# Decay attention: value product in two halves, diagonal block in two pairs, unread matmuls in the filling

## What is computed

```python
scores = jnp.einsum('bhqd,bhkd->bhqk', qh, k_rec) / math.sqrt(d)
t = jnp.arange(s, dtype=jnp.float32)
decay = jnp.exp(-LAMBDA_DECAY * jnp.abs(t[:, None] - t[None, :]))
scores = scores * decay[None, None, :, :]
attn = jax.nn.softmax(scores, axis=-1)
out = jnp.einsum('bhqk,bhkd->bhqd', attn, v_rec)
```

## Time and profile before

| | |
|---|---|
| median of 3 runs | 1181.23 us (1179.67 to 1182.42) |
| the profiled execution's own time | 1183.64 us |
| its span | 1181.8 us |
| PE busy | 1059.1 us (90%) |
| DVE busy | 768.1 us (65%) |
| ACT busy | 648.9 us (55%) |
| decay attention, filling to last step | 241 to 700 us of the span |

### The profile page before, as it was taken

How to read it: one execution, slowest core, us unless ns; L and a number is a source line. 1 busy time by engine, 2 the same in 40 slices (tenths; PEclk the granted TensorE clock), 3 DMA queues, 4 the chain that set the end, 5 groups by cost and what they waited for, 6 DMA issues and landing times.

```text
span 1181.8 us, 14237 instructions
## 1 busy us (share of the span) xinstructions
PE 1059.1 (90%) x5214; PEld 397.2 (34%) x5224; DVE 768.1 (65%) x1234; ACT 648.9 (55%) x1098; POOL 185.6 (16%) x107
## 2 busy tenths in 40 slices
PE   5899998985999999999999999998899758999998
PEld 2233333331233333333333334443343212344343
DVE  2678236368899999999998221026599998973200
ACT  4687455272277877877777652335744374413321
POOL 0222810033000000000000000000164313450000
PEclk9899999995599999999999999999899978999999
DMA  7000000069633032130000000000000000000000
GB/s 257 1 2 1 0 0 1 5 240 279 134 55 57 7 60 41 23 61 4 7 8 3 6 1 0 1 0 1 0 1 1 1 0 1 0 1 1 18 0 18
DMA packets 31194, 38.24 MB, mean 32 GB/s; under 512 B 7964, under 2 KB 22300, under 8 KB 30744
## 3 DMA queue, kind: packets, MB, share of 16 engines
q1 hardware_dynamic: 31128, 37.37, 12.5%
HBM read 23.23 MB, written 13.86 MB: 31 GB/s over the span
## 4 chain that ended last, share of the span: by engine, by line
PE 59%; ACT 11%; DVE 10%; issue 3%; DMA 1%; SPq 1%; ACTq 0%; DVEq 0%; POOL 0%; another core or an unknown queue 0%
PE PS L1437 17%; PE PS L1030 11%; PE PS L1014 8%; ACT arena L1039 6%; DVE ffn L926 3%; PE PS L1426 2%; PE PS L1446 2%; PE PS L1427 2%; PE PS L994 2%; DVE arena L1660 2%; PE PS L1071 1%; PE PS L916 1%; PE PS L1602 1%; PE PS L1612 1%; DVE arena L1543 1%
## 5 line engine op out<-in xcount | busy, mean ns | idle before, releaser
L926 DVE CUSTOM_DVE_ANT_0 ffn<-PS,XP 128x1024 bf16<-128x1024 f32 x256 | 305.2, 1219 | 20.1 <-PE PS L916 18.2
L1039 ACT ACTIVATE arena<-PS 128x384 f32<-128x384 f32 (+1 forms) x512 | 249.0, 544 | 117.4 <-PE PS L1014 114.6
L916 PE MATMUL PS<-arena 48*128 48x512 bf16 (+3 forms) x704 | 171.9, 346 | 13.3 <-DMA arena<-scr 8.4
L1014 PE MATMUL PS<-arena 50*128 50x512 bf16 (+3 forms) x640 | 158.0, 324 | 12.0 <-ACT arena L1039 4.9
L1030 PE MATMUL PS<-arena 128*32 128x512 f32 (+1 forms) x1280 | 139.1, 526 | 0.0
L1465 ACT ACTIVATE arena<-PS,w_scl 128x512 f32<-128x512 f32 x64 | 43.6, 687 | 158.0 <-PE PS L1437 157.9
L1437 PE MATMUL PS<-arena,w_h1T 128*128 128x512 f32 x256 | 118.2, 608 | 11.5 <-DVE arena L1475 6.6
L1437 PE MATMUL PS<-arena,w_h2T 128*128 128x512 f32 x256 | 114.9, 594 | 0.0
L1014 PEld LDWEIGHTS PS<-arena 50*128 50x128 bf16 x640 | 42.9, 95 | 155.3 <-ACT arena L1039 131.8
L1660 DVE TENSOR_TENSOR_SCAN arena<-arena 128x512 f32<-128x512 f32 x64 | 83.1, 1298 | 0.1
L1689 POOL TENSOR_TENSOR arena<-arena 128x512 f32<-128x512 f32 x32 | 58.6, 1830 | 155.5 <-DVE arena L1668 155.5
(11 more groups left out here) (219 smaller groups left out, 1530.4 us busy)
## 6 DMA issues: line engine op xcount, KB each, us to landing
arena<-scr SPq DMA_DIRECT2D x64, 192.0 KB, 5.7
scr<-arena SPq DMA_DIRECT2D x16, 384.0 KB, 5.4
scr<-arena SPq DMA_DIRECT2D x16, 256.0 KB, 4.8
scr<-arena SPq DMA_DIRECT2D x16, 128.0 KB, 3.0
XP<-xT SPq DMA_DIRECT2D x1, 1024.0 KB, 4.9
w_h1T<-h1T SPq DMA_DIRECT2D x1, 1024.0 KB, 6.8
w_h2T<-h2T SPq DMA_DIRECT2D x1, 1024.0 KB, 8.5
arena<-MH SPq DMA_DIRECT2D x64, 4.0 KB, 1.7
```

Of the source, the lines that this page charges most:

```text
L916: mm = t.matmul(PS[:, bank, k0 - lo:k1 - lo], packed(m, g, v, slice(q * P, (q + 1) * P), KP), packed(m, g, 2 + v, slice(k0, k1), KP), star ...
L926: v.tensor_tensor_reduce(JUNK[:, u % 2, :], PS[:, bank:bank + 2, :].rearrange("p a b -> p (a b)"), STRIP[:, at:at + S], 1.0, -3.0e38, ALU. ...
L1014: mm = t.matmul(PS[:, score_bank(T, i), at:at + b_ - a_], packed(n, g, 2 + v, slice(kt * P, (kt + 1) * P), KP + MROWS), packed(n, g, v, sl ...
L1039: nc.scalar.activation(PT[:, T % 2, score_head(T, i), a0_:a1_], PS[:, score_bank(T, i), a0_:a1_], ACT.Exp).then_inc(s_free, 1)
```

## The change

On PE, a step with units and no turn near it becomes: S0 U00 B01 S1 U01 PVa S2 U10 B23 S3 U11 PVb. PVa and PVb are the two halves of the value product by query columns (256 each, eight PE instructions each); only PVb waits for the diagonal's exponential, and the half that holds the diagonal block is always PVb (`value_halves`). In a turn the transpose comes after U10. In the step after a turn, `diag_pe` for that very step takes the places B01 and B23, and `diag_max_pe` comes behind PVb; `fix_dve` moves on DVE from the end of the turn's step to the start of the next, where nothing lies between the two places. From step 116 on: S0 B01 S1 S2 S3 B23, projections, PVa PVb.

`idle_pe` adds fp32 matmuls whose results nobody reads: 28 of 128x128 by 128 columns behind the preparation, before the wait for the packed operands, into bank 7; and 2 behind each of the 26 leading units, into `O_BANK`.

DVE's, ACT's and SP's instructions stay the same in number and kind.

```diff
@@ -1017,20 +1017,29 @@
                               start=True, stop=True, skip_group_check=True)
             mm.then_inc(s_s, 1)
 
-        def pv_pe(t, T):
+        def value_halves(T):
+
+            (a0_, b0_, q0_), *rest = layout(T)[3]
+            parts = ((a0_, b0_, q0_),) + tuple(rest) if rest else ((0, CH // 2, 0), (CH // 2, CH, CH // 2))
+            last = layout(T)[2]
+            return parts if last is None or last >= CH // 2 else parts[::-1]
+
+        def pv_pe(t, T, half):
             n, s = divmod(T, NS)
             hf, kt = s // NKT, key_tile(s)
-            t.wait_ge(s_free, GH * (T + 1))
-            if is_diag(T):
+            if half == 0:
+                t.wait_ge(s_free, GH * (T + 1))
+                if s % NKT == 0 and T > 0:
+                    t.wait_ge(o_free, 2 * n + hf)
+            elif is_diag(T):
                 t.wait_ge(dg_free, T // 2 + 1)
-            if s % NKT == 0 and T > 0:
-                t.wait_ge(o_free, 2 * n + hf)
-            for m, (a_, b_, q) in enumerate(layout(T)[3]):
-                for g in range(GH):
-                    mm = t.matmul(PS[32 * g:32 * g + 32, O_BANK, q:q + b_ - a_], VG[:, n % 2, kt, g, :],
-                                  PT[:, T % 2, g, a_:b_], start=(s % NKT == 0 and m == 0), stop=(s % NKT == NKT - 1),
-                                  skip_group_check=True)
-            mm.then_inc(pv_free, 1)
+            a_, b_, q = value_halves(T)[half]
+            for g in range(GH):
+                mm = t.matmul(PS[32 * g:32 * g + 32, O_BANK, q:q + b_ - a_], VG[:, n % 2, kt, g, :],
+                              PT[:, T % 2, g, a_:b_], start=(s % NKT == 0), stop=(s % NKT == NKT - 1),
+                              skip_group_check=True)
+            if half == 1:
+                mm.then_inc(pv_free, 1)
 
         def exp_act(a, T, i):
             e = GH * T + i
@@ -1102,12 +1111,19 @@
         LAST_SUMS, LN5_AT, SIXTH_FREE = NSTEP - 4, NSTEP - 9, NSTEP - 4
         RECIPROCAL_AT = 6
 
+        def idle_pe(t, times, bank):
+
+            for _ in range(times):
+                t.matmul(PS[:, bank, 0:P], ident[:], center[:], start=True, stop=True)
+
         def a1_pe(t):
             a1_prep_pe(t)
+            idle_pe(t, 28, 7)
             t.wait_ge(a1_v, 1 + NCH)
             for u in range(LEAD):
                 unit_pe(t, u, 0)
                 unit_pe(t, u, 1)
+                idle_pe(t, 2, O_BANK)
                 if u == NTH + 1:
                     maxima_pe(t, 0)
             diag_pe(t, 0, HEADS[0:2])
@@ -1131,27 +1147,22 @@
                     t.wait_ge(pk_m, 64 * (T // NKT + 1))
                 if s == 0:
                     t.wait_ge(vg_in, n + 1)
+                after_turn = T - 1 in TURNS
+
+                def block(heads):
+                    if after_turn:
+                        diag_pe(t, T, heads)
+                    elif turn is None:
+                        diag(heads)
                 scores_pe(t, T, 0)
                 unit(0, 0)
+                block(HEADS[0:2])
                 scores_pe(t, T, 1)
                 unit(0, 1)
                 if T >= RING:
                     scores_pe(t, T, 2)
                     scores_pe(t, T, 3)
-                if turn is not None:
-                    maxima_pe(t, turn)
-                elif T - 1 not in TURNS:
-                    diag(HEADS[0:2])
-                    diag(HEADS[2:4])
-                unit(1, 0)
-                if T < RING:
-                    scores_pe(t, T, 2)
-                unit(1, 1)
-                if T < RING:
-                    scores_pe(t, T, 3)
-                if T - 1 in TURNS:
-                    diag(HEADS[0:2])
-                    diag(HEADS[2:4])
+                    block(HEADS[2:4])
                 if T == SIXTH_FREE:
                     t.wait_ge(ln_free, 1 + late_count(LN5[0], 1))
                 if T == PROJ_FROM:
@@ -1159,10 +1170,22 @@
                 for c, a in PROJ_PE.get(T, ()):
                     project_pe(t, c, a)
                 if T > 0:
-                    pv_pe(t, T - 1)
-                if T in TURNS:
-                    diag(HEADS[0:2])
-                    diag(HEADS[2:4])
+                    pv_pe(t, T - 1, 0)
+                if T < RING:
+                    scores_pe(t, T, 2)
+                unit(1, 0)
+                if T < RING:
+                    block(HEADS[2:4])
+                if turn is not None:
+                    maxima_pe(t, turn)
+                if T < RING:
+                    scores_pe(t, T, 3)
+                unit(1, 1)
+                if T > 0:
+                    pv_pe(t, T - 1, 1)
+                if after_turn:
+                    diag_max_pe(t, T, HEADS[0:2])
+                    diag_max_pe(t, T, HEADS[2:4])
                 if T == LN5_AT:
                     t.wait_ge(x_ready, 1 + NCH * 4 + 2)
                     center_pe(t, LN5[0], 0, 6, XR)
@@ -1170,7 +1193,8 @@
                     variance_pe(t, LN5[0], 0, 6)
                 if T == LAST_SUMS:
                     last_sums_pe(t, 2)
-            pv_pe(t, NSTEP - 1)
+            pv_pe(t, NSTEP - 1, 0)
+            pv_pe(t, NSTEP - 1, 1)
             last_sums_pe(t, 3)
             project_pe(t, 3, 0)
             project_pe(t, 3, 1)
@@ -1214,6 +1238,8 @@
                 u = LEAD + 2 * T
                 if T in TURNS:
                     both_sides_dve(v, TURNS[T])
+                if T - 1 in TURNS:
+                    fix_dve(v, T)
                 if u < NUNIT:
                     unit_dve(v, u)
                 if T in TURNS:
@@ -1222,8 +1248,6 @@
                     fix_dve(v, T + 1)
                 if u < NUNIT:
                     unit_dve(v, u + 1)
-                if T in TURNS:
-                    fix_dve(v, T + 1)
                 if s == RECIPROCAL_AT and n > 0:
                     v.wait_ge(den_in, 16 * n)
                     v.reciprocal(RS, RS).then_inc(den_r, 1)
```

## The result

| | before | after |
|---|---|---|
| executions beside each other | 1179.67 to 1188.70, median 1181.23 (5) | 1164.99, 1166.51, 1190.05, 1190.45, 1193.80 (median 1190.05) |
| the profiled one: own time, span | 1183.64, 1181.8 | 1193.80, 1192.0 |
| instructions | 14237 | 16054 |

The changed kernel has two kinds of executions, 25 us apart. Two of five lie where the forecast was (1165); three lie where the rival "slower by the filling" was (1189). The ratio to the kernel before, which takes the shorter kind alone, is 0.9857 (95%: 0.9808 to 0.9905); by its median over all five the changed kernel is 0.7% slower than the kernel before. The profile caught one of the longer kind, so it shows both things at once: steps that became faster, and a filling that became much slower.

A forecast was written before the change was run, and what follows sets the result against it. A chain between PE and ACT holds the kernel, with DVE nearly full. 1183.6 - 11.9 (steps) - 4.4 (filling) = 1167.3 us for the profiled execution; the median lies 2.4 lower: 1165, range 1156 to 1178.

The forecast's parts named there:

- slower by the filling: Rival, chance 0.07: clock falls before 278 us and stays down, leading units take 1.9 against 1.15 us; 1189 us.
- The pair of steps: An odd and an even step between turns: repeats every 5.25 us against 5.56; bounds 5.20 and 5.45.
- Half a value product: PE time of one half of the split value product: 0.5 us plus 0.1 for getting in.
- slower by passages: Rival, chance 0.08: each half product costs x more than 0.6 us; at x = 0.25, 1198 us.
- The turn: Turn and step after it: fix waits 0.6 us, pair 6.55 against 6.47, cycle 22.30; 14 cycles give 11.9.
- The end: Steps 116 to 127, PE work and ACT waits: taken as 0 us, between -3 and +3.
- The filling: Unread matmuls around leading units keep the clock up through steps 0 to 2: 4.4 us gained, bounds 0 and 5.

The follow-up runs named there:

- the order alone: The changed kernel without both calls of `idle_pe`, so no unread matmuls: 1164.75 us, ratio 0.9852 to the kernel before.
- the filling alone: The kernel before plus only the two `idle_pe` calls: five executions of 1179.8 to 1186.9 us (ratio 1.0011), seven of 1201.9 to 1206.9.
- the block early in the step after a turn: The order alone with B23 of the step after a turn behind U01 instead of U10: 1164.08 us, ratio 0.9825.
- POOL in four: The order alone with POOL's normalisation multiply cut into four pieces of 256 columns: 1163.62 us, ratio 0.9845.
- The halves alone: The order alone with B01 and B23 side by side behind U01: 1182.92 us, ratio 1.0002.
- the pairs alone: The order alone with the value product whole behind U11, both halves side by side: 1187.14 us, ratio 1.0039.

## Why the prediction was right, and where it was not

The forecast of 1165 and the sum behind it (-16.3 us) fit the order alone and the shorter executions of the change. The other three executions, 1190 to 1194, lie outside its range of 1156 to 1178. Its terms do not all fit either, and that the sum comes out is in part luck.

**The pair of steps: right.** Forecast 5.25, measured 5.24 in the pair shown and 5.20 to 5.39 elsewhere. DVE waits for no unit any more; the pace is close to its own 5.20.

**Half a value product: right.** I took 0.6. The rows at 444.09 (first half, L1038) and 444.66 (S2) are 0.57 apart, so two halves take 1.14 where the whole took 1.0. The rival "slower by passages" needed 0.15 us more for a half than I took; it is 0.03 less.

**The turn: right in its place, a little off in size.** A new wait of 0.6 from L981 was forecast; 0.50 came, in every turn. A cycle was to take 22.30 and took 22.10 or 22.23, in the mean 22.17. Fourteen cycles gave 13.9 us (325.14 to 311.28) where I had 11.9. Of this, 1.2 come on top in the first cycle, which in the kernel before ran partly at the lower clock (24.26 us at 0.96) and in the order alone at the full one (22.09).

**The end: not seen.** I took 0, between -3 and +3. From the turn at step 115 to the last residual it takes 51.55 instead of 55.21 us, 3.7 less. Part of it is the clock: before, it is at 0.66 from 675 to 685 us, and in the order alone the whole stretch is at 0.97 (0.94 before). The other profiles tell the two apart. At the same mean clock of 0.94 the stretch takes 55.08 us with the filling alone and 53.18 with the block early in the step after a turn, so about 2 us are the order's own. At 0.97 it takes 51.5, and at 1.00 50.4 (changed kernel, POOL in four). The halves alone have 51.90 at 0.97, the pairs alone 54.13 at 0.94. The step that failed is that I let the savings and waits of this stretch cancel to 0.

```profile
675.00:685.00 10.00, 8.98 (x44) 3.27 (x48) 1.89 (x3) 6.46 (x15) 0.00 (x0) 0.66 0.01 2
```

**The filling: wrong.** It was to give 4.4 us. Without it the time is the same, and with it held up by 36 matmuls, 0.9 us came before step 3 (43.65 to 42.79) and none in the median. Two steps failed. The first is an arithmetic one: I put 28 matmuls at 7.4 us, by 1.05 us for eight instructions; but that row is a busy time with the tail of its last instruction in it (in the kernel with 36 ahead and none in the units, the same row of 1.06 starts at 268.83 and the next work at 269.72, 0.89 later). 56 in a row take 6.42, 0.115 each. So they end 1.64 us before the operands instead of 1.0, and by the forecast's own words PE "would be busy without a gap" was false in either case. The second is the assumption that a clock which holds through the leading units holds through steps 0 to 2; PE is idle there for 0.6 of 2 us at first (308 to 310), and the clock fell at about 312. With four more matmuls in step 0 it held, in the one execution that was profiled.

**The rival by the filling: right in mechanism and size, wrong in its chance.** The clock fell, a unit took 2.12 (forecast 1.9), and the executions are 1190 to 1194 (forecast 1189). I gave it 0.07; it was 3 of 5 executions, 7 of 12 in the old order. What spoke for it stood in the trace before: 8.44 us of idleness, then 31 us at 0.50 with PE busy for 26. I weighed it as one outcome of the kernel, where it is one outcome of an execution. That two of five came out near 1165, and not none as with 20 matmuls ahead, was chance.

**The sum.** The order alone against before, by spans: -1.3 (the operands came earlier, which is no doing of the order), +1.1 (first unit to step 3, whose cause was not looked for), -13.9 (turns), -3.7 (end), -0.3 (the rest): -18.1. The forecast had -11.9, -4.4 and 0. It came out near the shorter executions because a gain at the end that it did not see stands in for a gain in the filling that was not there.

## What to carry to other kernels

A long block on an in-order engine hurts by what waits behind it: cut it so that each piece fits into a wait that is there anyway. Check that the engine has room for it, and try such edits together as well as alone: here each of two gained nothing without the other, by my reading because one makes the room that the other needs. Work that only keeps a clock up must cover the idle time to its end, and perhaps the first waits of the next stage as well; where it sits in a loop, price it at the lower level too, because that is what it costs in the executions where the cover fails. A gap of nearly the same length (1.60 and 1.64 us) gave either kind of execution, so time such an edit in more than a few of them.

## What the runs showed of the hardware

The clock did not come back for some 65 us under load. In the changed kernel PE is busy for 58.25 of 59 us from 286 on and stays at 0.50, with short fp32 matmuls and bf16 halves of 512 columns by turns; in the order alone PE is busy for 25.3 of 30 us at 0.50. With 36 ahead the same mix of matmuls ran for 30 us at 1.00. This mix thus runs at either level, and which one it was depended here on the idle time ahead of it. The clock came back only in the steps: 0.50 from 345 to 346, 0.80 from 346 to 350, 1.00 in the cycles behind. The Trainium skill, "TensorE: Matmul & The Clock Gate", Part 1, says that a busy stretch brings the higher level back; by that rule most of the leading units would have run at full clock again. The trace does not agree. Whether the kind of the matmuls is why was not tried.

DVE's copy of 128x32 fp32 stands still beside POOL's multiply, until the latter's end. Four instances, each with POOL's end and the copy's: 415.17 and 415.20; 387.81 and 387.85 (36 ahead); 387.44 and 387.47, 521.02 and 521.05 (order alone). A reduction that begins beside the same instruction keeps its time (order alone: 1.22 us at 385.53, POOL from 385.07 to 387.44). The Trainium skill, "SBUF — State Buffer", Who interferes with whom, says that the two engines share a pair of ports, which whoever issues first holds for its whole instruction, and that copies may take that pair; these rows agree, and POOL's instruction began first in all four. A copy 1.8 us late cost the cycle 2.7 us, and in the kernel with 36 ahead a copy 1.1 us late was followed by the lower clock:

```profile
388.00:390.00 2.00, 1.79 (x21) 0.63 (x20) 1.97 (x5) 1.09 (x2) 0.00 (x0) 1.00 0.00 0
390.00:396.00 6.00, 5.68 (x46) 1.78 (x44) 4.19 (x8) 3.16 (x6) 0.00 (x0) 0.51 0.03 6
396.00:400.00 4.00, 4.00 (x33) 1.18 (x29) 2.91 (x6) 2.13 (x4) 0.00 (x0) 0.50 0.00 0
```

Its cycle took 26.71 us. In the order alone copies 0.50 and 0.57 us late gave cycles of 22.61 and 22.68. Where one copy falls was thus worth from some 0.5 to 4.5 us of an execution, against a cycle of 22.17; how much of the spread of 9 us of the order alone it makes is not shown.
